# Variances of the input rows from squares and one-column products instead of transposes and BN_STATS, in the opening of a language-model tower kernel

## The reference

```python
x = emb[tokens]                                  # 8 rows x 512 tokens, 128 channels
x = x + _fast_memory(x, mask, W_upd, b_upd, W_f, b_f, decay_param)   # a scan over the tokens
x = _ln(x, norm_g, norm_b)                       # variance over the 128 channels
for i in range(4):
    h = _ln(x, cms_ln_g[i], cms_ln_b[i])
    h = gelu(h @ cms_W1[i] + cms_b1[i])          # 128 -> 512
    x = x + h @ cms_W2[i] + cms_b2[i]            # 512 -> 128
```

## Time and profile before

| | us |
|---|---|
| median of 3 runs | 415.62 (415.4 to 415.87) |
| the profiled execution | 415.76 |
| its span, first to last instruction | 413.9 |
| first product of `up(0)` starts, from the span's start | 45.66 |
| PE busy of the span | 389.1 (94%) |
| DVE, ACT, POOL busy | 350.8, 324.6, 260.3 |

### The profile page before, as it was taken

One profiled execution on the slowest core, in us unless ns is written; L12 is line 12 of the kernel. 1 busy time (PEld: TensorE's weight loads), 2 busy tenths in 40 slices (PEclk: granted clock), 3 DMA queues, 4 the chain that ended last, 5 costly groups with the idle time before them and its releaser, 6 DMA issues.

```text
span 413.9 us, 6363 instructions
## 1 busy us (share of the span) xinstructions
PE 389.1 (94%) x1988; PEld 313.9 (76%) x1988; DVE 350.8 (85%) x850; ACT 324.6 (78%) x555; POOL 260.3 (63%) x389
## 2 busy tenths in 40 slices
PE   5798879999999999999999998999997999998996
PEld 2586568888888888888888887877875877785773
DVE  4887689888988888898888979999987899889885
ACT  1263588999999988898887765578787999996993
POOL 0575787787778779877788466586521765343552
PEclk9999999999999999999999999999999999999999
DMA  6900010222132222212222000000000000000001
GB/s 205 357 3 0 2 25 27 53 52 47 31 51 52 34 46 52 51 34 44 52 50 52 1 1 2 1 2 1 2 2 1 1 2 13 15 13 13 14 13 26
DMA packets 15849, 14.94 MB, mean 36 GB/s; under 512 B 9796, under 2 KB 10568, under 8 KB 15560
## 3 DMA queue, kind: packets, MB, share of 16 engines
q1 hardware_dynamic: 15816, 14.54, 14.4%
HBM read 13.42 MB, written 1.11 MB: 35 GB/s over the span
## 4 chain that ended last, share of the span: by engine, by line
PE 70%; DVE 17%; ACT 5%; issue 5%; POOL 1%; DMA 1%; SPq 1%; POOLq 0%; DVEq 0%; ACTq 0%
PE ps L1497 62%; PE ps L1520 5%; DVE hid L1379 2%; ACT w_all L869 1%; DVE stats L999 1%; PE ps L1528 1%; ACT x L863 1%; DVE x L1379 1%; DVE hh L1280 1%; DVE kstat L1220 1%; DVE x L1236 1%; PE ps L1703 1%; DMA xn<-in_w_f 1%; DVE qmax L1232 1%; DVE qsum L1246 1%
## 5 line engine op out<-in xcount | busy, mean ns | idle before, releaser
L704 ACT ACTIVATE hid<-ps,b_fold 128x512 f32<-128x512 f32 x128 | 84.0, 681 | 21.3 <-PE ps L1497 20.9
L1073 DVE TENSOR_TENSOR hid_lo<-hid,hid_hi 128x1024 fp32r<-128x1024 f32 x64 | 78.7, 1229 | 25.4 <-ACT hid_hi L709 25.1
L1497 PE MATMUL ps<-xn_hi,w_all 128*128 128x512 f32 x256 | 87.4, 402 | 0.6 <-DVE xn_lo L1068 0.6
L1497 PE MATMUL ps<-hid_hi,w_all 128*128 128x512 f32 x256 | 85.0, 393 | 0.0
L709 ACT ACTIVATE hid_hi<-hid 128x1024 fp32r<-128x1024 f32 x64 | 67.9, 1061 | 2.0
L1497 PEld LDWEIGHTS ps<-xn_hi,w_all 128*128 128x128 f32 x256 | 48.4, 189 | 10.8 <-issue 0.9
L1497 PEld LDWEIGHTS ps<-hid_hi,w_all 128*128 128x128 f32 x256 | 48.1, 188 | 9.9
L1497 PE MATMUL ps<-xn_lo,w_all 128*128 128x512 f32 x128 | 49.9, 390 | 0.0
L1497 PE MATMUL ps<-hid_lo,w_all 128*128 128x512 f32 x128 | 49.8, 389 | 0.0
L1497 PE MATMUL ps<-hid_hi,ew 128*128 128x512 f32 x131 | 41.4, 402 | 0.7 <-ACT memT L807 0.4
L999 DVE BATCH_NORM_STATS2 stats<-ps 128x6 f32<-128x128 f32 x160 | 35.2, 281 | 2.8 <-PE ps L1520 2.8
(11 more groups left out here) (231 smaller groups left out, 913.0 us busy)
## 6 DMA issues: line engine op xcount, KB each, us to landing
rstd_row<-roots SPq DMA_DIRECT2D x29, 256.0 KB, 3.7
hh<-in_tokens SPq DMA_DIRECT2D x8, 256.0 KB, 7.9
hid<-in_w SPq DMA_DIRECT2D x1, 1024.0 KB, 7.2
rstd_row<-in_w SPq DMA_DIRECT2D x1, 1024.0 KB, 10.2
out<-hh SPq DMA_DIRECT2D x7, 128.0 KB, 2.0
ew_raw<-in_expert_w SPq DMA_DIRECT2D x1, 512.0 KB, 9.8
roots<-rstd SPq DMA_DIRECT2D x29, 2.0 KB, 1.4
ew_raw<-in_expert_w SPq DMA_DIRECT2D x1, 256.0 KB, 9.9
```

Of the source, the lines that this page charges most:

```text
L704: act.activation(hid[:, j % 2, f, :], bank[f], ACT.Gelu, bias=b1_fold[:, j // B * F + f:j // B * F + f + 1]).then_inc(gelu_done, 1)
L1073: dve.tensor_tensor(hid_lo[:, j % 2, 2 * p:2 * p + 2, :], hid[:, j % 2, 2 * p:2 * p + 2, :], hid_hi[:, j % 2, 2 * p:2 * p + 2, :].bitcast( ...
L1497: return pe.matmul(out, lhsT, rhs, start=start, stop=stop)
```

## The change

- The variance of an input row no longer comes from turning the row. ACT squares the row after `pre(n)` (`square`, into `hid[:, 1]`, four buffers), and PE sums the squares over the partitions with four one-column products (`squares_sum`): the squares are the stationary operand, a column of twos the moving one. DVE brings the four columns from `TB` to `var_x` with one small instruction (`input_variance`), and POOL needs one instruction a row for the root (`inverse_root_of_input`).
- PE's order in a lap: look-ups first, then the broadcast, then the sum of squares, then folds. `broadcast(n - 3)` and `norm(n - 3)` stand in each lap from 3 on.
- Two useless products instead of three at a time, and none in laps 4 to 7; those ahead of the laps and behind them stay.
- Folds, `w1_hi`, `w2_hi` and `w2_lo` have other places; at the end of the opening PE now has the broadcast of ffn 0, the sum of squares of row 7, the broadcast of row 5 and then `centre_w1(1)`, and ACT has `w1_hi(1)`, `w2_hi(2)` and `w2_hi(3)` ahead of `xhi(0)`.

```diff
-REPEATS = 3
+REPEATS = 2
...
+        var_x = sb("var_x", [P, B, NT])
...
+        squares = hid[:, 1, :, :]
...
+        squared = sem("rows_squared")
...
-            def inverse_root_of_pair(n):
-
-                pool.wait_ge(stats_ready, n + 2 + FREE)
-                st, vi = stats6[:, n % 4:n % 4 + 2, :, :], var_in[:, n % 4:n % 4 + 2, :, :]
...
-                twos = two[:, :].unsqueeze(1).broadcast_to([P, 2, NT])
-                pool.tensor_tensor(rstd[:, n % 4:n % 4 + 2, :], vi[:, :, 0, :], twos, ALU.mult).then_inc(rstd_ready, 2)
+            def inverse_root_of_input(n):
+
+                place = place_in(n)
+                pool.wait_ge(stats_ready, place + 1 + FREE)
+                pool.tensor_tensor(rstd[:, place % 4, :], var_x[:, n, :], mhalf[:, 0:NT],
+                                   ALU.pow).then_inc(rstd_ready, 1)
...
             pool.wait_ge(onehot_dve, POOL_ROWS[0])
-            for n in POOL_ROWS[0:3]:
-                one_hot(n)
+            one_hot(POOL_ROWS[0])
+            one_hot(POOL_ROWS[1])
             pool.wait_ge(mhalf_set, 1)
-            inverse_root_of_pair(0)
+            inverse_root_of_input(0)
+            one_hot(POOL_ROWS[2])
+            inverse_root_of_input(1)
+            inverse_root_of_input(2)
             one_hot(POOL_ROWS[3])
-            inverse_root_of_pair(2)
+            inverse_root_of_input(3)
+            inverse_root_of_input(4)
+            inverse_root_of_row(place_ffn(0), place_ffn(0) % 4)
+            inverse_root_of_input(5)
             pool.wait_ge(ld["w2"], 16)
             w2_lo(0)
-            inverse_root_of_pair(4)
-            inverse_root_of_pair(6)
+            inverse_root_of_row(place_ffn(1), place_ffn(1) % 4)
+            inverse_root_of_input(6)
             w2_lo(1)
-            inverse_root_of_pair(8)
-            for n in range(place_in(B - 1), B * (L + 1)):
+            inverse_root_of_row(place_ffn(2), place_ffn(2) % 4)
+            inverse_root_of_input(7)
+            w2_lo(2)
+            for n in range(B + 3, B * (L + 1)):
                 inverse_root_of_row(n, n % 4)
-                if n in (place_in(B - 1), B + 3):
-                    w2_lo(2 + (n == B + 3))
+                if n == B + 3:
+                    w2_lo(3)
                 if n == B + 2 * B + 4:
...
+            def square(n):
+
+                act.wait_ge(pre_ready, n + 1)
+                if n >= F:
+                    act.wait_ge(x_t, place_in(n - F) + 1)
+                act.activation(squares[:, n % F, :], x[:, n, :], ACT.Square).then_inc(squared, 1)
+
             def w1_in(l):
...
             decays(0)
-            for n in range(B):
+            decays(1)
+            for n in range(1, B):
+                square(n - 1)
                 if n + 1 < B:
                     decays(n + 1)
                 if n == 3:
                     act.wait_ge(ld["w1"], 16)
                     w1_in(0)
                     w1_in(1)
-                if n == 4:
+                if n >= 4:
+                    affine(n - 4)
+                if n in (4, 5):
+                    w1_in(n - 2)
+                if n == 6:
+                    w1_hi(0)
                     act.wait_ge(ld["w2"], 16)
                     w2_hi(0)
+                if n == 7:
                     w2_hi(1)
-                if n >= 4:
-                    affine(n - 4)
-                if n == 4:
-                    w1_in(2)
-                if n == 5:
-                    w1_in(3)
-                    w1_hi(0)
-                if n == 6:
-                    w2_hi(2)
-                    w2_hi(3)
+            square(B - 1)
+            affine(4)
             w1_hi(1)
-            affine(4)
+            w2_hi(2)
+            w2_hi(3)
...
+            def input_variance(n):
+
+                dve.wait_ge(x_t, place_in(n) + 1)
+                dve.tensor_scalar(var_x[:, n, :], bank[TB][:, 0:NT], 0.5 / D, EPS, ALU.mult,
+                                  ALU.add).then_inc(stats_ready, 1)
+
             def one_hot(n):
...
                     one_hot(6)
-                if n in (6, 7):
-                    norm(2 * n - 10)
+                pre(n)
                 if n >= 1:
-                    row_stats(place_in(n - 1) % 4, place_in(n - 1) + 1)
-                pre(n)
-                if n == 7:
-
-                    dve.wait_ge(folds_done, 1)
-                    dve.tensor_tensor(eb1_fold[:, :], bank[5][:, L * F:L * F + E], cols[:, C_EB1:C_EB1 + E], ALU.add)
-                    dve.tensor_tensor(br_fold[:, :], bank[5][:, L * F + E:L * F + 2 * E], rows[:, R_BR:R_BR + E], ALU.add)
-                    dve.tensor_tensor(b1_fold[:, :], bank[5][:, 0:L * F], cols[:, C_B1:C_B1 + L * F],
-                                      ALU.add).then_inc(folds_ready, 1)
-                if n in (4, 5, 6):
-                    norm((0, 1, 3)[n - 4])
+                    input_variance(n - 1)
+                if n >= 3:
+                    norm(n - 3)
                 if n in (5, 6):
                     row_stats(place_ffn(n - 5) % 4, place_ffn(n - 5) + 1)
             w1_lo(0)
+
+            dve.wait_ge(folds_done, 1)
+            dve.tensor_tensor(eb1_fold[:, :], bank[5][:, L * F:L * F + E], cols[:, C_EB1:C_EB1 + E], ALU.add)
+            dve.tensor_tensor(br_fold[:, :], bank[5][:, L * F + E:L * F + 2 * E], rows[:, R_BR:R_BR + E], ALU.add)
+            dve.tensor_tensor(b1_fold[:, :], bank[5][:, 0:L * F], cols[:, C_B1:C_B1 + L * F],
+                              ALU.add).then_inc(folds_ready, 1)
...
             norm(5)
-            row_stats(place_in(7) % 4, place_in(7) + 1)
+            input_variance(7)
             w1_lo(1)
...
+            def squares_sum(n):
+
+                pe.wait_ge(squared, n + 1)
+                pe.wait_ge(stats_ready, place_in(n) + FREE)
+                for t in range(NT):
+                    last = mm(bank[TB][:, t:t + 1], squares[:, n % F, t * P:(t + 1) * P], two[:, 0:1])
+                last.then_inc(x_t, 1)
+
             def broadcast(slot, n):
...
             keep_clock_at(0, bank[5])
+            pe.wait_ge(mhalf_set, 1)
             for n in range(1, B):
-                turn(x[:, n - 1, :], pre_ready, n, place_in(n - 1))
                 look_up_embedding(n)
-                if n in (6, 7):
-                    broadcast(place_in(2 * n - 10) % 4, place_in(2 * n - 10))
                 if n + 1 < B:
                     look_up(n + 1)
-                if n in (4, 5):
-                    broadcast(n - 4, n - 4)
-                if n <= 4:
+                if n >= 3:
+                    broadcast((n - 3) % 4, n - 3)
+                squares_sum(n - 1)
+                if n <= 3:
                     keep_clock_at(n, bank[5])
-                if n == 7:
-                    pe.wait_ge(scanned, 7 + FREE)
-                    keep_clock_at(n, bank[2])
                 if n == 3:
                     pe.wait_ge(ld["w1"], 16)
                 if 3 <= n < 3 + L:
                     bias_fold(n - 3)
-                if n == 6:
-                    broadcast(3, 3)
                 if n == 4:
                     for name in ("ew1", "wr"):
                         pe.wait_ge(ld[name], 16)
-                    expert_fold((0, 1))
-                if n == 5:
-                    expert_fold((2, 3, 4))
-                if n == 6:
-                    expert_fold((5, 6, 7), router=True)
+                    expert_fold((0, 1, 2))
                 if n == 6:
                     centre_w1(0)
-                if n == 7:
-                    broadcast(place_ffn(0) % 4, place_ffn(0))
                 if n >= 5:
                     turn(x[:, n - 5, :], x0_ready, n - 4, place_ffn(n - 5))
-                if n in (5, 6):
-                    keep_clock_at(n, bank[5])
+                if n == 5:
+                    expert_fold((3, 4))
+                if n == 7:
+                    expert_fold((5, 6, 7), router=True)
+            broadcast(place_ffn(0) % 4, place_ffn(0))
+            squares_sum(B - 1)
+            broadcast(place_in(5) % 4, place_in(5))
             centre_w1(1)
-            broadcast(place_in(5) % 4, place_in(5))
-            turn(x[:, B - 1, :], pre_ready, B, place_in(B - 1))
             keep_clock_at(B - 1, bank[2])
```

More of the change, by code:

```diff
@@ L480, in w2_lo @@
                                    w_all[:, l, 1, :, 0, :], ALU.subtract).then_inc(w2_lo_ready, 1)
-            def inverse_root_of_pair(n):
-                pool.wait_ge(stats_ready, n + 2 + FREE)
-                st, vi = stats6[:, n % 4:n % 4 + 2, :, :], var_in[:, n % 4:n % 4 + 2, :, :]
-                own.inc(pool.tensor_tensor(vi[:, :, 0, :], st[:, :, :, 1], st[:, :, :, 4], ALU.subtract))
-                v = own.inc(pool.tensor_tensor(vi[:, :, 1, :], st[:, :, :, 2], st[:, :, :, 5], ALU.add))
-                own.wait(v)
-                v = own.inc(pool.tensor_scalar(vi[:, :, 1, :], vi[:, :, 1, :], 4.0 / D, 4.0 * EPS, ALU.mult, ALU.add))
```

(11 more changed lines are left out.)

## The result

| | before | after |
|---|---|---|
| median, us | 415.75 (415.4 to 415.94, 4 runs) | 430.29 (429.88 to 435.82, 4 runs) |
| the profiled execution, span | 415.76, 413.9 | 435.82, 434.0 |
| `pre(7)` ends | 41.45 | 50.93 |
| first product of `up(0)` | 45.66 | 64.03 |

The ratio is 1.0373, 95% interval 1.0318 to 1.0429: 14.5 us slower, where 1.1 was forecast and the range ended at 419.2. The profiled execution is the longest of the four; `up(0)` starts 18.4 us later in it, and its span is 20.1 longer. In all that follows the ratios leave out runs over 1.5% above the fastest of their kernel, while medians and ranges are of all runs.

The account below looks back on a forecast made before the run. The opening bounds the kernel, through its laps and a tail before up(0). pre(7) ends 4.0 us earlier, the tail takes 9.4 instead of 4.2, so up(0) starts 1.1 later: 416.8 us, range 415.0 to 419.2.

Parts of the forecast that it names:

- walk of laps and tail: Opening, piece by piece: pre(7) ends at 37.4 us, the tail takes 9.4, up(0) starts at 46.8 instead of 45.66.
- the tail: From pre(7) to up(0): PE waits for statistics ahead of row 7's squares; 9.4 us instead of 4.2.
- tokens of row 6: Lap 2: the one-hot awaits tokens by DMA, so pre(2) ends between 18.7 and 19.3; 19.2 taken, 0.8 won.
- price of a one-column sum: A sum of squares on PE costs 0.88 us, taken from the bias fold; bounds 0.41 and 0.99.
- rival 1: One-column sums on PE are cheap: at 0.41 each, up(0) at 44.5 and 414.4 us, faster; chance 0.12.
- Laps 3 to 6: PE is the bound: laps of 3.39, 3.65, 3.81 and 4.27 us, together 15.1, ending at 34.4.
- rival 2: The clock falls at PE's waits of 1.9 and 2.8 us before up(0): +3 to +4, 420 to 421; chance 0.12.
- by their absence: Laps 3 to 6: useless products that go, 0.73 us a time, were counted only as PE time no longer spent.

Follow-up runs that it names:

- e10: Changed kernel with sums of 128 columns and useless products where PE waits in lap 7 and the tail, order kept; 417.41 us, ratio 1.003.
- e11: Changed kernel with 128-column sums, centre_w1(1) before row 7's squares, w2_hi(2) and w2_hi(3) behind xhi(0), useless products in PE's waits; 414.82 us.
- e5: Changed kernel with the moving operand of the sums of squares 64 columns wide instead of one; 421.89 us, ratio 1.013.
- e9: Kernel before with each group of three useless products replaced by four one-column fp32 products with the identity; 431.42 us.
- e12: Kernel before with each group of three useless products replaced by four 128-column fp32 products with the identity; 416.3 us, ratio 0.9995.
- e13: Kernel before without any of the useless products, nothing in their place; 425.07 us, ratio 1.0163.
- e1: Changed kernel with the useless products of the kernel before: three at a time, in laps 1 to 7; 434.67 us, ratio 1.0435.
- e6: Changed kernel with the moving operand of the sums of squares 128 columns wide instead of one; 420.88 us, ratio 1.0099.
- e3: Kernel before with useless products thinned as in the change: two at a time, none in laps 4 to 7; 416.21 us, ratio 1.0012.
- e2: Changed kernel with three useless products instead of two at each place, in no further lap; 431.67 us, ratio 1.0357.

## Why the prediction was wrong

- **The walk of laps and tail was right, for a clock of 1.00.** e10 is the change at that clock, with wider sums and useless products in its waits: `pre(7)` 0.4 earlier than forecast, the tail 9.57 us for 9.4, `up(0)` 0.2 earlier. From broadcast to broadcast its laps 3 to 6 take 3.36, 3.78, 4.04 and 3.76 us, 14.9 for the 15.1 of the sum. Its median, 417.41, is 1.7 above before where I had 1.1. That remaining 0.6 stays open. One candidate is the tokens of row 6, which let `pre(2)` end at 18.47 in e10's profile and at 19.98 in e11's, with the same work ahead of it. The prediction's bounds for it, 18.7 and 19.3, were too narrow: in after, DVE waits for these tokens until 18.45 and `pre(2)` ends at 19.59. So part of e10's nearness is luck, since its laps began 0.7 early.
- **The price of a one-column sum was right** (0.81 for 0.88), and rival 1 falls: eight records of one column take no less time than eight of 64 or 128 (ahead of useless products 0.81 in after, 0.81 from 20.59 to 21.40 in e5, 0.82 from 19.75 to 20.57 in e10).
- **The step that failed is "Laps 3 to 6": "PE has more, and is the bound", summed at the prices of the earlier trace rows, all of which are of clock 1.00.** The sum took it for granted that a busy PE keeps that clock. I asked about the clock only in rival 2, and looked there for waits. The fall came at some 21 us, in the laps, where PE was about to be busy without a gap, and its laps took 6.1 to 7.5 us for 3.4 to 4.3. What the laps lack is columns: the turn's four pieces of 128 went, and most useless products, and time of PE full of one-column products came. e5 against after shows it by one operand's width (8.4 us), and so do e9 and e12 without the change; leaving the useless products out of before costs 9.2 us (e13).
- **It may have fed itself.** PE bounds the changed laps at either clock, so a fall makes them longer for the same columns, and the clock of after stays low for 27 us. That this keeps it low is argued, not shown.
- **Columns alone do not order all the runs.** Lap 4 of e1 has 3510 columns in 4.41 us (23.12 to 27.53) and the clock falls behind it; lap 4 of e5 has 2574 in 3.74 us (22.73 to 26.47) and the clock holds until 39 us. e1 has the more columns by either count, and the more time in products of one column. What mix of the two brings a fall stays open.
- **Rival 2 existed, on top.** e6 has its two waits, a fall right behind each (at 42.9 and 49.8 us), and e10 fills them: 420.88 less 417.41 is 3.5 us, where I had said 3 to 4. Its chance of 0.12 was too low, because I read the earlier trace rows, one wait of 1.67 among dense 512-column work, as proof for waits among thin work; e6's first wait is no longer, 1.67, and the clock falls behind it.
- **The account of the 14.5 us**, by medians: 1.7 for laps and tail at full clock (e10), 3.5 for the fall in the tail (e6 less e10), 1.0 from 128 to 64 columns (e5 less e6, little more than their scatter), 8.4 from 64 columns to one (after less e5). Sum 14.6, as it must be, since each step starts where the last one ends: it splits the loss and does not confirm it. The medians are from different sets of runs, so each is good to some 0.5 us at best.
- **The thinning of the useless products by itself cost nothing that can be told** (e3), beside turns that stay. Giving them back to the changed kernel gained nothing (e1, e2), yet before cannot do without them all (e13). I costed them as time of PE alone, counted "by their absence".

The Trainium skill's page "TensorE: Matmul & The Clock Gate", in "Part 1: The HAM clock gate", says that the gate follows how busy PE has been recently. The granted clock here does not follow the busy time that the profile shows: 6.00 of 6.00 at 0.50 in after, 3.71 of 6.00 at 1.00 in e3, 4.06 of 6.00 at 0.72 in e13. From 13 to 19 us PE is busy for 5.58 of 6.00 in e9 and 5.35 in e12, and it is e9's clock that falls, at 19.3 us.

## What to carry to other kernels

When a change takes columns from PE or fills its time with products of few columns, price the stage at both clocks, even if PE's row in the profile will be full: busy time is no evidence that the clock holds. Widening the moving operand to 64 or 128 columns costs hardly any time per product and kept the clock in the laps, where more useless products, which cost time on a PE that is the bound, did not. When a walk shows new waits of PE beside thin work, cost the fall of the clock in the forecast, not as a remote rival, and fill the waits with columns.

## What the hardware showed that was not expected

- The same slots of PE's time, filled with one-column products, with 128-column ones, or left empty: 431.42, 416.3 and 425.07 us. The busiest of the three (5.58, 5.35 and 4.06 of 6.00 from 13 to 19 us) was not the one that kept its clock; that thin work does worse than none is not shown, since the ranges of the first and the last overlap.
- The eight fp32 records of a sum ahead of useless products take 0.81 us at one column, 0.81 at 64 and 0.82 at 128 (start to next start, clock 1.00). Each has a weight load of 128x128, 191 ns on average in after's first two sums. Up to 128 columns come free there. Ahead of a bias fold it is 0.84 at 64 (23.94 to 24.78 in e5) and 0.89 at 128 (24.36 to 25.25 in e6).
- At the lower clock the one-column products take twice as long too (1.57 us), not only those that stream many columns.
